# A mixing and convolution kernel: the order and queue of its first loads, dummy matmuls, and an early table load

## The chip, the cores and the metric

The kernel runs on one core of one Trainium2 chip. The metric is the device time of one execution in microseconds. A core has five engines with instruction streams of their own (TensorE for matmuls, VectorE, ScalarE, GpSimd, and SyncE, here only an issuer of DMAs) and 16 DMA engines that all its queues share.

## The reference

The reference has two layers, each added to its input. The first mixes channels with one of 16 weight matrices, chosen for each batch element. The second is a long convolution along time whose kernel comes from 64 complex exponentials per channel.

```python
# x: (64, 128, 2048) float32; 16 weight matrices of (128, 128)
W = weights[condition]                        # condition: (64,) in 0..15
x = x + einsum('bct,bcd->bdt', x, W)
dt = exp(log_dt); A = -exp(log_A_real) + 1j * A_imag; dtA = A * dt[:, None]
Ct = (C[..., 0] + 1j * C[..., 1]) * (exp(dtA) - 1.0) / A
K = 2.0 * einsum('hn,hnl->hl', Ct, exp(dtA[:, :, None] * arange(2048))).real
y = causal_convolution(x, K)                  # by FFT in the reference
x = x + (y + x * D[:, None]) * (arange(2048) < length[:, None])[:, None, :]
```

## The kernel before, in words

The work has two phases. In the **mixing phase** a loop runs over the 64 batch elements ("samples"). For each, 1 MB of x is loaded (`x_f`, six buffers), multiplied on TensorE by a weight matrix with the identity added (`w_buf`, six buffers), copied in reversed order by ScalarE from PSUM to `stage` (four buffers), and stored to the scratch tensor `u_scratch` in DRAM. In the **second phase**, 64 pairs of channels are read back, and the convolution is made of matmuls with small Toeplitz matrices and a state of the exponentials. The second phase begins when the stores of all samples are done, but for some rows of the last four.

Each engine's stream is written out by hand, and they meet at semaphores. What matters for the first 60 us:

- **SyncE** (SP) issues, in this order, six loads for the natural parameters (`nat`, semaphore `s_in[0]`), the selector `cond_sb` (`s_in[3]`), `logs` (`s_in[1]`), the first six loads of x, two of `len_i` and one of `d_col` (`s_in[4]`). Then for each sample n it issues the load of sample n + 5 (from n = 1), waits for ScalarE's copies of sample n, and issues the store of sample n. So the seventh load of x stands behind the first store.
- **ScalarE** (ACT) issues the load of all weights, `w_f` (1 MB, `s_in[2]`). Then its loop waits for a sample's matmuls and for a free `stage`, and copies in two halves. After sample 4 it computes sines (`waves_of_turns`) for which it waits on VectorE (`s_turn`). Its table load is put in by the compiler ahead of the first activation.
- **GpSimd** (POOL) builds `ident` (which raises `s_const` to 2) and other constants. Then, after `w_f` and `cond_sb` are there, it reads the selector of each sample and adds the identity to its weight matrix, into `w_buf` (L348). At sample 30 it waits for `s_tab`, VectorE's tables, and builds some matrices ahead of the next `w_buf`.
- **TensorE** waits for `ident` and for the six `nat` loads, transposes four blocks (L392), and from then on mixes. Sample 1 waits, in addition, until VectorE has copied the four transposed blocks (`s_dve` at 4). From sample 30 on, five samples have small matmuls (`taps`, L400) ahead of their own, for which `s_tab` is needed. A sample's four float32 matmuls (L418) leave eight records in the trace.
- **VectorE** waits for the transposes, copies them (L643, L645), and then works through a long chain of small operations (the exponentials, powers and tables) until `s_tab` at L786, during the samples 0 to 29.

ScalarE's and SyncE's DMAs go to different queues: those of SyncE to q1, those of ScalarE to q10, GpSimd's to q0. The 16 DMA engines serve all.

Of the kernel before, what the change touches and what calls it, by code (L numbers as in the profile page):

```python
# [6 lines left out]
F32 = mybir.dt.float32  # L7
# [4 lines left out]
ACT = mybir.ActivationFunctionType  # L12

P = 128
NB, H, T = 64, 128, 2048
NC = 16
NM = 64
Q = 256
NJ = T // Q
JJ = 2  # L20
# [13 lines left out]

TAPS = 30
PIECES = 5
WAVES = 4
XS = 6
STAGES = 4
# [8 lines left out]
def ap(t, offset, dims, parts=P, first=0):  # L48

    width = 1  # L50
    for n in t.shape[1:]:
        width *= n
    return bass.AP(t, offset + first * width, [[width, parts]] + [list(d) for d in dims])


def build(nc, x, cond, length, w_in, log_dt, c_in, log_a, a_im, d_in, out):
# [6 lines left out]
    with ctx:  # L63
        def sb(name, shape, dt, where=ctx):
            return where.enter_context(nc.sbuf_tensor(name, shape, dt))
# [5 lines left out]
        cond_sb = sb("cond_sb", [1, NB], I32)  # L71
        len_i = sb("len_i", [P, 1], I32)
# [2 lines left out]
        row_f = sb("row_f", [P, 1], F32)  # L75
        pad = sb("pad", [P, 8], F32)
        d_col = sb("d_col", [P, 1], F32)
        ident = sb("ident", [P, P], F32)
        eyes = sb("eyes", [P, 2, NM], F16)
        lam_v = sb("lam_v", [P, H, 2, 2], F16)  # L80
# [31 lines left out]
        nat = [sb(f"nat{i}", [P, 2 * P], F32, making) for i in range(3)]  # L112
        logs = sb("logs", [P, 2, H], F32, making)
# [26 lines left out]
        bank = ctx.enter_context(nc.psum_tensor("bank", [P, 8, 512], F32))  # L140
# [55 lines left out]

        @block.sync
        def _(sp):
            sp.dma_start(nat[0][:, 0:NM], log_a[:, :]).then_inc(s_in[0], 16)
            sp.dma_start(nat[0][:, NM:P], log_a[:, :]).then_inc(s_in[0], 16)  # L200
            sp.dma_start(nat[1][:, 0:NM], a_im[:, :]).then_inc(s_in[0], 16)
            sp.dma_start(nat[1][:, NM:P], a_im[:, :]).then_inc(s_in[0], 16)
            sp.dma_start(nat[2][:, 0:P], c_in.rearrange("h n c -> h (n c)")).then_inc(s_in[0], 16)
            sp.dma_start(nat[2][:, P:2 * P], c_in.rearrange("h n c -> h (n c)")).then_inc(s_in[0], 16)
            sp.dma_start(cond_sb[:, :], cond.rearrange("(a b) -> a b", a=1)).then_inc(s_in[3], 16)
            sp.dma_start(logs[:, 0, :], log_dt.partition_broadcast(P)).then_inc(s_in[1], 16)

            def load_x(n):
                wait(sp, s_mm, n - XS + 1)
                sp.dma_start(x_f[n % XS][:, :], x[n, :, :]).then_inc(s_x[n % XS], 16)  # L210

            def store_u(n, first, last, s):
                dst = bass.AP(u_dram, first * ROWS * NG * Q + n * NG * Q,
                              [[ROWS * NG * Q, last - first], [NB * NG * Q, JJ], [1, NG * Q]])
                sp.dma_start(dst, stage[n % STAGES][first:last, :, :, :].rearrange("p j a t -> p j (a t)"))\  # L215
                    .then_inc(s, 16)

            for n in range(XS):
                load_x(n)
            for j in range(JJ):  # L220
                sp.dma_start(len_i[j * NB:(j + 1) * NB, :], length.rearrange("(b a) -> b a", a=1),
                             allow_slow_non_contiguous=True).then_inc(s_in[4], 16)
            sp.dma_start(d_col[:, :], d_in.rearrange("(h a) -> h a", a=1)).then_inc(s_in[4], 16)
            for n in range(NB):
                if 1 <= n <= NB - XS:
                    load_x(n + XS - 1)
                sp.wait_ge(s_ev, 2 * (n + 1))
                if n < NB - LATE:
                    store_u(n, 0, H, s_us[n % STAGES])
                else:  # L230
                    store_u(n, 0, EARLY, s_early)

            def load_u(i, c, h):
                wait(sp, s_ov, 4 * (UN * i + c - 4) + 2 * h + 2)
                sp.dma_start(u_row[c % 4][:, h, :, :].rearrange("p g q -> p (g q)"),  # L235
                             bass.AP(u_dram, (2 * (UN * i + c) + h) * (ROWS * NG * Q), [[NG * Q, ROWS], [1, NG * Q]]))\
                    .then_inc(s_row[c % 4][h], 16)

            def load_toeplitz(i, c):
                wait(sp, s_out, 4 * (UN * i + c - 3))  # L240
                src = bass.AP(k_dram, (UN * i + c) * (4 * KROW), [[1, P], [KROW, 4], [1, Q]])
                sp.dma_start(toep[c % 4][:, :, :, :].rearrange("p h a t -> p (h a) t"), src)\
                    .then_inc(s_t[c % 4], 16)

            def transpose_g(i, c):

                for lo in (0, NM):
                    sp.dma_start(gt_sb[c % 2][:, :, :, :, lo:lo + NM].rearrange("p h a b m -> p (h a b) m"),  # L248
                                 g_sb[c % 4][NM - lo:P - lo, :, :, :].rearrange("p h a t -> p (h a t)"),
                                 transpose=True).then_inc(s_gt[c % 2], 16)  # L250

            def store_out(i, c, h):
                o = 2 * (c % 2) + h
                sp.wait_ge(s_ov, 4 * (UN * i + c) + 2 * h + 2)
                for j in range(JJ):
                    dst = bass.AP(out.tensor, (2 * (UN * i + c) + h) * T + j * Q,
                                  [[H * T, NB], [JJ * Q, NG], [1, Q]])
                    sp.dma_start(dst, o_sb[o][j * NB:(j + 1) * NB, :, :]).then_inc(s_store[o], 16)

            sp.wait_ge(s_g, 1)  # L260
            transpose_g(0, 0)
            sp.wait_ge(s_kd, 80)
            for r in range(STAGES):
                sp.wait_ge(s_us[r], 16 * len(range(r, NB - LATE, STAGES)))
            sp.wait_ge(s_early, 16 * LATE)
            for c in range(2):
                for h in range(2):
                    load_u(0, c, h)
                load_toeplitz(0, c)

            def slot(i, c):
                if c == EARLY // 2 - 2:
                    sp.wait_ge(s_late, 16 * LATE)
                if has(i, c + 2):
                    load_u(i, c + 2, 0)
                if has(i, c + 1):

                    wait(sp, s_st, 7 * (UN * i + c) - 6)
                    sp.sem_inc(s_go, 1)
                    sp.wait_ge(s_g, UN * i + c + 2)  # L280
                    sp.sem_inc(s_go, 1)
                    transpose_g(i, c + 1)
                if has(i, c - 2):
                    store_out(i, c - 2, 1)
                if has(i, c + 2):
                    load_u(i, c + 2, 1)
                    load_toeplitz(i, c + 2)
                if c == 0:
                    for n in range(NB - LATE, NB):
                        store_u(n, EARLY, H, s_late)  # L290
                if has(i, c - 1):
                    store_out(i, c - 1, 0)

            slots(sp, slot)
            for o in range(4):
                sp.wait_ge(s_store[o], 32 * (PAIRS // 2))
# [87 lines left out]

        @block.tensor
        def _(pe):
            pe.wait_ge(s_const, 2)
            pe.wait_ge(s_in[0], 96)
            srcs = [nat[0][:, 0:P], nat[1][:, 0:P],
                    ap(nat[2], 0, [[P, 2], [2, NM]]), ap(nat[2], 1, [[P, 2], [2, NM]])]  # L390
            for k, src in enumerate(srcs):
                last = pe.transpose(bank[:, 4 + k, 0:P], src, ident[:, :])  # L392
            last.then_inc(s_tr, 1)

            def taps(piece, b):
                if piece == 0:
# [8 lines left out]

            for n in range(NB):
                if n == 1:
                    pe.wait_ge(s_dve, 4)
                wait(pe, s_ev, 2 * (n - 1))
                piece = n - TAPS  # L410
                if 0 <= piece < PIECES:
                    taps(piece, 4 * (n % 2))
                pe.wait_ge(s_x[n % XS], 16 * (n // XS + 1))
                pe.wait_ge(s_w, n + 1)
                for k in (1, 2, 3, 0):
                    if k == 0 and 0 <= piece < PIECES:
                        pe.wait_ge(s_kl, piece + 1)
                    last = pe.matmul(bank[:, 4 * (n % 2) + k, :], w_buf[n % XS][:, :],  # L418
                                     x_f[n % XS][:, k * 512:(k + 1) * 512], start=True, stop=True)
                last.then_inc(s_mm, 1)  # L420
# [98 lines left out]

        @block.scalar  # L520
        def _(act):
            act.dma_start(w_f[:, :, :], w_in.rearrange("s c d -> c s d")).then_inc(s_in[2], 16)

            def waves_of_turns():
                act.wait_ge(s_turn, 1)
# [369 lines left out]
```

## Time and profile before

| | |
|---|---|
| median of 3 runs | 1099.62 us (1095.68 to 1100.15) |
| the profiled execution | 1099.54 us, its span 1097.7 us |
| mean granted TensorE clock | 0.984 |
| busy shares of the span | PE 91%, PEld 67%, DVE 70%, ACT 50%, POOL 46% |
| HBM read, written | 152.37 MB, 134.41 MB |

The span is what the profiler saw from the first to the last instruction; the execution's own time is 1.84 us longer. PE is TensorE's matmul, PEld its weight load, DVE is VectorE, ACT ScalarE, POOL GpSimd, SPq the issuing of DMAs on SyncE. Matmuls are pipelined and their ends are modelled, so starts and the distances between them are the better measure. The DMA share of a stretch is the mean over 16 engines and can exceed 1 by a little, since packets overlap.

### The profile page before, as it was taken

Reading aid. Unit: us, or ns where it says so; the run is one execution under the profiler, and the core shown is the slowest. Engines: PE = TensorE matmul, PEld = TensorE weight load, DVE = VectorE, ACT = ScalarE, POOL = GpSimd, SP = SyncE. Lnnn points to the kernel's source line nnn. Section 1 sums busy time; section 2 is a strip of 40 time slices with the busy share of each in tenths; the row PEclk is TensorE's granted clock in tenths of the full one; section 3 lists DMA queues with packets and bytes.
Section 4 is the critical chain, followed back from the end, with each engine's and each line's share of the span. In section 5 each row is a group of like instructions: output and inputs, shape, how many; then the busy total and the mean of one; then the engine's idle time right before and its main releaser. Section 6 shows DMA issues by size and latency. Waiting matters only on the chain.

```text
span 1097.7 us, 29010 instructions
## 1 busy us (share of the span) xinstructions
PE 996.0 (91%) x11526; PEld 731.3 (67%) x11526; DVE 770.1 (70%) x1710; ACT 547.3 (50%) x1163; POOL 502.4 (46%) x542
## 2 busy tenths in 40 slices
PE   6987789677756999999999999999999999999997
PEld 2332244232224788888888888888888888888886
DVE  6989920000004888888888888888888888888885
ACT  2633344334332555555555555555555555555553
POOL 2111043000204466656656656556666566565530
PEclk9999999999997999999999999999999999999999
DMA  9999999999989899999999999999999999999994
GB/s 334 415 425 421 425 421 423 376 424 424 423 320 312 179 220 249 228 218 234 215 234 230 222 238 225 221 232 218 239 229 226 235 230 229 226 226 234 221 214 117
DMA packets 220311, 305.48 MB, mean 278 GB/s; under 512 B 79938, under 2 KB 178626, under 8 KB 211986
## 3 DMA queue, kind: packets, MB, share of 16 engines
q1 hardware_dynamic: 219490, 302.37, 97.6%
q8 instruction: 94, 1.54, 0.6%
q10 hardware_dynamic: 528, 1.05, 0.4%
q14 instruction: 39, 0.32, 0.1%
q0 software_dynamic: 160, 0.20, 0.1%
HBM read 152.37 MB, written 134.41 MB: 261 GB/s over the span
## 4 chain that ended last, share of the span: by engine, by line
PE 67%; DMA 25%; ACT 4%; SPq 2%; issue 1%; DVE 1%; ACTq 0%
DMA u_scratch<-stage 24%; PE bank L479 15%; PE bank L488 15%; PE bank L444 13%; PE bank L430 10%; PE bank L456 7%; PE bank L485 5%; ACT stage L554 3%; PE bank L418 2%; DVE x_t L831 1%; DMA x_f<-in_x 1%; SPq L248 1%; SPq L215 0%; SPq L235 0%; DVE st_sb L821 0%
## 5 line engine op out<-in xcount | busy, mean ns | idle before, releaser
L479 PE MATMUL bank<-toep,u_t 128*128 128x192 f16 (+1 forms) x3072 | 344.7, 220 | 0.4
L816 DVE SCALAR_TENSOR_TENSOR u_t<-bank,u_t 128x512 f16<-128x512 f32 x256 | 176.3, 688 | 193.9 <-ACT u_t L567 191.8
L488 PE MATMUL bank<-g_sb,st_sb 128*128 128x256 f16 x1536 | 307.4, 274 | 0.0
L418 PE MATMUL bank<-x_f,w_buf 128*128 128x512 f32 x512 | 240.7, 618 | 64.1 <-ACT stage L554 52.7
L430 PE MATMUL bank<-ident,u_row 128*128 128x128 f32 x1024 | 280.9, 279 | 11.7 <-DMA u_row<-u_scratch 11.1
L575 ACT ACTIVATE st_sb<-bank 128x128 f16<-128x128 f32 x448 | 123.8, 276 | 289.2 <-PE bank L456 199.5
L479 PEld LDWEIGHTS bank<-toep,u_t 128*128 128x128 f16 x3072 | 232.0, 99 | 14.9 <-issue 0.4
L418 PEld LDWEIGHTS bank<-x_f,w_buf 128*128 128x128 f32 x512 | 95.8, 195 | 204.7 <-issue 110.6
L846 DVE COPY_PREDICATED o_sb<-mask,u_row 128x512 f32<-128x512 uint8 x256 | 205.7, 803 | 16.6 <-issue 16.6
L554 ACT ACTIVATE stage<-bank 128x1024 f32<-128x1024 f32 x128 | 123.9, 1021 | 174.0 <-DMA u_scratch<-stage 156.8
L485 PE MATMUL bank<-toep,x_t 128*128 128x64 f16 x2048 | 189.0, 193 | 0.3 <-issue 0.3
L340 POOL TENSOR_TENSOR lam_sb<-eyes,lam_v 128x512 f16<-128x512 f16 x64 | 75.5, 1179 | 238.2 <-PE bank L456 238.2
L567 ACT ACTIVATE u_t<-bank 128x512 f16<-128x512 f32 x256 | 152.2, 595 | 59.2 <-PE bank L430 48.5
L821 DVE TENSOR_TENSOR st_sb<-bank,st_sb 128x128 f16<-128x128 f32 x448 | 129.6, 289 | 57.3 <-ACT st_sb L575 53.6
L430 PEld LDWEIGHTS bank<-ident,u_row 128*128 128x128 f32 x1024 | 146.3, 144 | 21.4 <-issue 13.1
L485 PEld LDWEIGHTS bank<-toep,x_t 128*128 128x128 f16 x2048 | 158.2, 98 | 0.5 <-issue 0.4
L444 PE MATMUL bank<-u_t,gt_sb 128*128 128x448 f16 x768 | 156.0, 353 | 0.2
L583 ACT ACTIVATE o_sb<-bank 128x512 f32<-128x512 f32 x256 | 153.3, 599 | 4.1 <-PE bank L488 4.0
L488 PEld LDWEIGHTS bank<-g_sb,st_sb 128*128 128x128 f16 x1536 | 149.6, 98 | 6.2
L456 PE MATMUL bank<-st_sb,lam_sb 128*128 128x64 f16 x2304 | 130.8, 193 | 9.6 <-DVE st_sb L821 9.2
L348 POOL TENSOR_TENSOR w_buf<-w_f,ident 128x128 f32<-128x128 f32 x64 | 33.1, 521 | 221.1 <-PE bank L418 215.6
L456 PEld LDWEIGHTS bank<-st_sb,lam_sb 128*128 128x128 f16 x2304 | 107.9, 98 | 38.3 <-issue 14.9
(122 smaller groups left out, 842.9 us busy)
## 6 DMA issues: line engine op xcount, KB each, us to landing
x_f<-in_x SPq DMA_DIRECT2D x64, 1024.0 KB, 19.6
u_row<-u_scratch SPq DMA_DIRECT2D x128, 512.0 KB, 5.8
out<-o_sb SPq DMA_DIRECT2D x256, 256.0 KB, 4.0
u_scratch<-stage SPq DMA_DIRECT2D x60, 1024.0 KB, 17.7
toep<-k_scratch SPq DMA_DIRECT2D x64, 256.0 KB, 5.6
u_scratch<-stage SPq DMA_DIRECT2D x4, 896.0 KB, 10.2
gt_sb<-g_sb SPq DMA_TRANSPOSE x128, 5.3
u_scratch<-stage SPq DMA_DIRECT2D x4, 128.0 KB, 4.7
```

What stands on the lines that cost most here:

```text
L418: last = pe.matmul(bank[:, 4 * (n % 2) + k, :], w_buf[n % XS][:, :], x_f[n % XS][:, k * 512:(k + 1) * 512], start=True, stop=True)
L430: last = pe.transpose(bank[:, 4 + q, g * P:(g + 1) * P], u_row[c % 4][:, h, g, tb * P:(tb + 1) * P], ident[:, :])
L444: last = pe.matmul(bank[:, h, 0:(NJ - 1) * NB], gt_sb[c % 2][:, h, a, 1 - tb, :], u_t[c % 4][:, h, tb, b, 0:(NJ - 1) * NB], start=(m == 0) ...
L456: last = pe.matmul(bank[:, h, j * NB:(j + 1) * NB], lam_sb[c % 2][:, h, a, :, :].rearrange("p k m -> p (k m)"), st_sb[c % 2][:, h, b, j * ...
L479: pe.matmul(bank[:, y, col + tb * P + NM:col + Q], u[:, h, tb, a, rows_], t[:, h, b, NM:Q - tb * P], start=first, stop=False, skip_group_c ...
L485: pe.matmul(bank[:, y, col + tb * P:col + tb * P + NM], x_t[c % 2][:, h, tb, rows_], t[:, h, b, 0:NM], start=False, stop=False, skip_group ...
L488: last = pe.matmul(bank[:, y, col:col + Q], st[:, h, a, gr * ROWS:(gr + 1) * ROWS], g[:, h, b, :], start=False, stop=(m == 2), skip_group_ ...
L554: act.activation(stage[n % STAGES][:, j, :, :].rearrange("p a (b t) -> p a b t", t=P), mixed[:, j, :, :, ::-1], ACT.Copy).then_inc(s_ev, 1)
L567: act.activation(u_t[c % 4][:, q // 2, q % 2, 0, :], bank[:, 4 + q, :], ACT.Copy, scale=US)\
L583: act.activation(o_sb[o][:, 2 * (v % 2):2 * (v % 2) + 2, :].rearrange("p g t -> p (g t)"), bank[:, 2 + v % 2, :], ACT.Copy, scale=1.0 / (U ...
L816: dve.scalar_tensor_tensor(out=t[:, q // 2, q % 2, 1, :], in0=bank[:, 4 + q, :], scalar=US, in1=t[:, q // 2, q % 2, 0, :], op0=MUL, op1=SU ...
L846: dve.copy_predicated(o_sb[2 * (c % 2) + v // 2][:, g2, :].rearrange("p g (b t) -> p (g b) t", t=P), mask[:, g2, :].rearrange("p g (b t) - ...
```

## The change

The loads of the small inputs leave SyncE's stream, so that the six loads of x are its first. ScalarE issues them all: `cond_sb` first, then `w_f`, then the rest in their old order. TensorE no longer begins with the transposes: it waits for `ident` only, runs 16 matmuls of `ident` with itself into a PSUM bank that nobody reads, mixes sample 0, and transposes ahead of sample 1. ScalarE gets an activation of one column that nobody reads, behind its DMAs, so that its table is loaded there.

```diff
+RUNUP = 16
@@ allocations
+        act_in = sb("act_in", [P, 1], F32)
@@ def _(sp)
-            sp.dma_start(nat[0][:, 0:NM], log_a[:, :]).then_inc(s_in[0], 16)
...
-            sp.dma_start(nat[2][:, P:2 * P], c_in.rearrange("h n c -> h (n c)")).then_inc(s_in[0], 16)
-            sp.dma_start(cond_sb[:, :], cond.rearrange("(a b) -> a b", a=1)).then_inc(s_in[3], 16)
-            sp.dma_start(logs[:, 0, :], log_dt.partition_broadcast(P)).then_inc(s_in[1], 16)
@@ behind the six load_x(n)
-            for j in range(JJ):
-                sp.dma_start(len_i[j * NB:(j + 1) * NB, :], length.rearrange("(b a) -> b a", a=1),
-                             allow_slow_non_contiguous=True).then_inc(s_in[4], 16)
-            sp.dma_start(d_col[:, :], d_in.rearrange("(h a) -> h a", a=1)).then_inc(s_in[4], 16)
@@ def _(pe)
             pe.wait_ge(s_const, 2)
-            pe.wait_ge(s_in[0], 96)
-            srcs = [nat[0][:, 0:P], nat[1][:, 0:P],
-                    ap(nat[2], 0, [[P, 2], [2, NM]]), ap(nat[2], 1, [[P, 2], [2, NM]])]
-            for k, src in enumerate(srcs):
-                last = pe.transpose(bank[:, 4 + k, 0:P], src, ident[:, :])
-            last.then_inc(s_tr, 1)
+            for _ in range(RUNUP):
+                pe.matmul(bank[:, 0, 0:P], ident[:, :], ident[:, :], start=True, stop=True)
@@ the loop over samples
             for n in range(NB):
                 if n == 1:
+                    pe.wait_ge(s_in[0], 96)
+                    srcs = [nat[0][:, 0:P], nat[1][:, 0:P],
+                            ap(nat[2], 0, [[P, 2], [2, NM]]), ap(nat[2], 1, [[P, 2], [2, NM]])]
+                    for k, src in enumerate(srcs):
+                        last = pe.transpose(bank[:, 4 + k, 0:P], src, ident[:, :])
+                    last.then_inc(s_tr, 1)
                     pe.wait_ge(s_dve, 4)
@@ def _(act)
+            act.dma_start(cond_sb[:, :], cond.rearrange("(a b) -> a b", a=1)).then_inc(s_in[3], 16)
             act.dma_start(w_f[:, :, :], w_in.rearrange("s c d -> c s d")).then_inc(s_in[2], 16)
+            act.dma_start(nat[0][:, 0:NM], log_a[:, :]).then_inc(s_in[0], 16)
...
+            act.dma_start(logs[:, 0, :], log_dt.partition_broadcast(P)).then_inc(s_in[1], 16)
+            for j in range(JJ):
+                act.dma_start(len_i[j * NB:(j + 1) * NB, :], length.rearrange("(b a) -> b a", a=1),
+                              allow_slow_non_contiguous=True).then_inc(s_in[4], 16)
+            act.dma_start(d_col[:, :], d_in.rearrange("(h a) -> h a", a=1)).then_inc(s_in[4], 16)
+
+            act.wait_ge(s_const, 2)
+            act.activation(act_in[:, :], ident[:, 0:1], ACT.Copy)
```

## Rows read from the trace of the kernel before

**Rows 1.** The page: DMA share and rate in 40 slices, and the chain by line.

```profile
DMA  9999999999989899999999999999999999999994
GB/s 334 415 425 421 425 421 423 376 424 424 423 320 312 179 220 249 228 218 234 215 234 230 222 238 225 221 232 218 239 229 226 235 230 229 226 226 234 221 214 117
...
DMA u_scratch<-stage 24%; PE bank L479 15%; PE bank L488 15%; PE bank L444 13%; PE bank L430 10%; PE bank L456 7%; PE bank L485 5%; ACT stage L554 3%; PE bank L418 2%; DVE x_t L831 1%; DMA x_f<-in_x 1%; SPq L248 1%; SPq L215 0%; SPq L235 0%
```

**Rows 2.** Stretches: busy time (instructions) of each engine, granted clock, DMA share, GB/s.

```profile
1.00:2.00 1.00, 0.00 (x0) 0.00 (x0) 0.00 (x0) 0.00 (x0) 0.59 (x4) 1.00 0.10 22
2.00:3.00 1.00, 0.00 (x0) 0.00 (x0) 0.00 (x0) 0.00 (x0) 0.65 (x7) 1.00 0.65 78
3.00:8.00 5.00, 0.00 (x0) 0.00 (x0) 0.00 (x0) 0.00 (x0) 1.66 (x8) 1.00 1.02 289
8.00:20.00 12.00, 9.63 (x17) 4.38 (x18) 9.51 (x27) 1.77 (x2) 3.35 (x7) 1.00 1.01 421
...
22.00:30.00 8.00, 8.00 (x20) 3.61 (x19) 7.68 (x7) 4.80 (x6) 1.42 (x3) 1.00 0.95 320
```

**Rows 3.** Timeline to 24 us: start, duration, engine, line, operation.

```profile
0.81 0.85 ACTq L522 DMA_DIRECT2D w_f<-in_L_cond_weights  x1
...
4.33 2.80 SPq L210 DMA_DIRECT2D x_f<-in_x  x6
...
9.21 0.45 POOL L348 TENSOR_TENSOR w_buf<-w_f,ident 128x128 f32<-128x128 f32 x1 [3.77 <-issue]
9.60 0.29 DVE L643 COPY logs<-bank 128x128 f32<-128x128 f32 x1 [9.60 <-PE bank L392]
...
11.46 24.05 PE L418 MATMUL bank<-x_f,w_buf 128*128 128x512 f32 x48 [1.90 <-DMA x_f<-in_x]
...
18.22 1.28 ACT L554 ACT_TABLE_LOAD   x1 [17.45 <-PE bank L418]
...
21.48 0.60 SPq L215 DMA_DIRECT2D u_scratch<-stage  x1
...
21.99 1.49 DVE L660 TENSOR_TENSOR waves<-waves,wide 128x1152 f32<-128x1152 f32 x1
```

**Rows 4.** Issues from 0 to 20 us: the last number is us to landing.

```profile
w_f<-in_L_cond_weights ACTq DMA_DIRECT2D x1, 0.5 KB, 6.9
```

**Rows 5.** DMA queues from 3 to 5, 5 to 7 and 8 to 20 us: packets, MB, share.

```profile
q10 hardware_dynamic: 297, 0.61, 97.4%
q1 hardware_dynamic: 5, 0.00, 0.3%
...
q10 hardware_dynamic: 213, 0.41, 74.0%
q1 hardware_dynamic: 447, 0.15, 34.4%
...
DMA packets 701, 5.05 MB, mean 421 GB/s; under 512 B 75, under 2 KB 85, under 8 KB 85
```

**Rows 6.** PE in one stretch (clock before the share), and the first matmuls.

```profile
42.00:43.00 1.00, 1.00 (x3) 0.50 1.09 459
...
8.47 1.09 PE L392 MATMUL bank<-ident,nat 128*128 128x128 f32 x4 [8.47 <-DMA nat<-in_L_cond_C]
```

**Rows 7.** The chain in order of time: start, duration, what.

```profile
41.09 5.41 PE bank L418 x8
```

**Rows 8.** Timelines from 138 to 163 us, of GpSimd and TensorE.

```profile
138.72 0.68 POOL L359 MEMSET st_sb<- 128x256 f16 x2 [13.30 <-DVEq L786]
...
148.03 0.86 POOL L348 TENSOR_TENSOR w_buf<-w_f,ident 128x128 f32<-128x128 f32 x2
...
157.29 1.76 PE L400 MATMUL bank<-beta_re,k_lhs 128*16 128x16 f32 x64
```

**Rows 9.** Issues from 60 to 300 us: the last number is us to landing.

```profile
u_scratch<-stage SPq DMA_DIRECT2D x48, 1024.0 KB, 17.7
...
k_scratch<-k_body POOLq DMA_DIRECT2D x4, 32.0 KB, 6.9
```

More of the change, by code:

```diff
@@ L198, in _ @@
         def _(sp):
-            sp.dma_start(nat[0][:, 0:NM], log_a[:, :]).then_inc(s_in[0], 16)
[L200 to L203, printed above, removed]
-            sp.dma_start(nat[2][:, P:2 * P], c_in.rearrange("h n c -> h (n c)")).then_inc(s_in[0], 16)
-            sp.dma_start(cond_sb[:, :], cond.rearrange("(a b) -> a b", a=1)).then_inc(s_in[3], 16)
-            sp.dma_start(logs[:, 0, :], log_dt.partition_broadcast(P)).then_inc(s_in[1], 16)
             def load_x(n):
@@ L521, in _ @@
         def _(act):
+            act.dma_start(cond_sb[:, :], cond.rearrange("(a b) -> a b", a=1)).then_inc(s_in[3], 16)
             act.dma_start(w_f[:, :, :], w_in.rearrange("s c d -> c s d")).then_inc(s_in[2], 16)
+            act.dma_start(nat[0][:, 0:NM], log_a[:, :]).then_inc(s_in[0], 16)
+            act.dma_start(nat[0][:, NM:P], log_a[:, :]).then_inc(s_in[0], 16)
+            act.dma_start(nat[1][:, 0:NM], a_im[:, :]).then_inc(s_in[0], 16)
+            act.dma_start(nat[1][:, NM:P], a_im[:, :]).then_inc(s_in[0], 16)
+            act.dma_start(nat[2][:, 0:P], c_in.rearrange("h n c -> h (n c)")).then_inc(s_in[0], 16)
+            act.dma_start(nat[2][:, P:2 * P], c_in.rearrange("h n c -> h (n c)")).then_inc(s_in[0], 16)
+            act.dma_start(logs[:, 0, :], log_dt.partition_broadcast(P)).then_inc(s_in[1], 16)
[5 more added lines that the diff above has]
+            act.activation(act_in[:, :], ident[:, 0:1], ACT.Copy)
             def waves_of_turns():
```

## The prediction

> **What bounds the kernel now.** First the page's chain, with its line of DMA busy shares and the rates below it [rows 1]. A quarter of the span (24%) hangs on stores of the stage, and the tenths of the DMA line stand at 9 for the first eleven slices of 27.4 us, some 300 us. So the mixing phase is bound by the 16 DMA engines (the later phase, where the DMA rate is near 230 GB/s, by TensorE). A change to the first 30 us can help only by filling time in which the DMA engines are not at full rate.
>
> The table by stretches says how much of that there is [rows 2]. Full rate is about 424 GB/s. From 0 to 8 us 1.54 MB were moved (0.022 + 0.078 + 5 x 0.289), where full rate gives 3.39 MB: 4.4 us lost. About 2 us of it are the start, before any packet; most of the rest is the price of small packets, with the engines busy (share 1.02 from 3 to 8 us), and stays with the bytes. Only the shares missing from 1 to 3 us (0.90 and 0.35) can be shortened. From 22 to 30 us the rate is 320: 104 x 8 / 424 = 1.97 us lost. The slices after it stand at 415 to 425, with few exceptions late in the phase.
>
> The timeline says why there is a hole at 22 us [rows 3]. The six loads of x are issued by 7.1 us and, by the rate, used up about 22.4 us. The next ones stand in SP's queue behind the first store, at 21.48. Before that store lie eight matmul records from 11.46 to 18.2, ScalarE's table load of 1.28 us and its copies of 1.94 us (19.5 to 21.48, less the handing over). Later a sample takes TensorE about 3.45 us ((24.05 - 6.8) / 5, from the 48 records) and the DMA engines 2 x 1.049 MB / 424 = 4.94 us, so a queue builds up behind them.
>
> **The change part by part.**
>
> *Loads of x first.* SyncE's first issue is at about 0.8 us, as w_f's on ScalarE. The first packet of any kind comes near 1.9 us (share 0.10 from 1 to 2 us), and those of x are of 8 KB, so the engines fill at once: of the missing 0.90 and 0.35 about 0.4 us is won (bounds 0 and 0.7). All the bytes stay, so the queue runs dry at 22.4 - 0.4 = 22.0 us.
>
> *The small loads on ScalarE.* Here I see the price. No sample starts without the weights: w_f landed at 7.71 (0.81 + 6.9 [rows 4]), and GpSimd had the first w_buf at 9.66 [rows 3], 1.95 us later. Before the change w_f met almost no rival: from 3 to 5 us its queue q10 had 297 packets in 97.4% of the time, 2 x 16 x 0.974 / 297 = 0.105 us each, and q1 had 5 [rows 5]. Afterwards q1 is full of 8 KB packets of x, each 0.315 us (12 x 16 x 1.01 / 616: the 701 of 8 to 20 us less 85 small ones [rows 5], with the share of [rows 2]). How two queues share an engine is what the sum hangs on. Nearest is the stretch from 5 to 7 us: both queues have packets and both move (213 and 447, the latter small), and q10 falls from 297 to 213. I take turns packet by packet. w_f has 512 / 16 = 32 packets on each engine, so it needs 32 x (0.105 + 0.315) = 13.4 us from about 3 us, or 12.4 if part of the small packets' cost hides under the large ones. I take 13, and half a microsecond to the landing: w_f lands at 16.5 us, with bounds 7.7 (undisturbed) and 21 (only when the x loads have let go, near 22). First matmul: 16.5 + 1.95 = 18.4 us against 11.46.
>
> The Trainium skill, page "DMA: Bandwidth & Descriptors", section "Queues, rings and completion order", says that each engine goes round robin between the queues that it has work for, a packet at a time. By that rule the landing is this 16.5 and the time this forecast; sharing in equal bytes would land w_f near 8.6 us and give the first rival's time. In no row of before do both queues have large packets, so this trace neither confirms nor refutes it.
>
> *16 matmuls on ident.* Ident is there within the first 2 us. A mixing matmul leaves two records, so these are 32; each takes between 0.21 us (a quarter of the 0.85 us spacing from 11.46 to 18.2, where a record has 512 columns) and 0.27 us (the four transposes with ident, 1.09 us [rows 6]). They end between 8 and 11 us. Only TensorE stands behind them, and it waits longer for the weights, so they cost nothing. They pay only if the clock is still up at 18.4 us. After a pause of 2.15 us the granted clock was 0.50 from 42 to 43 us (1.2 GHz) [rows 6], and eight records took 5.41 us instead of 3.45 [rows 7]. The pause here is 7 us or more. I count the clock as fallen: 6.1 us for the first sample (bounds 5.4 and 6.8, the two cold samples of before). It ends at 24.5.
>
> [...]
>
> *Table fetched early.* 1.28 us leave the path of the first store [rows 3]. ScalarE has 12 DMAs to issue ahead of it, one at 0.85 and eleven at about 0.47 (2.80 / 6 [rows 3]), 6.0 us; the table comes at about 9 and is needed at 24.5: hidden. First store: 24.5 + 0.1 + 1.94 = 26.5 us against 21.48.
>
> *Transposes moved behind sample 0.* They wait for six small loads queued behind w_f on q10, some 16 packets beside the last of x, then the rest, about 21.5 us: hidden under sample 0. Then 1.1 us of transposes [rows 6] and four vector copies of about 0.33 us (0.29 and a gap), now on TensorE's path: 2.4 us, in which nothing else can run there. Sample 1 goes from 26.9 to 30.3, its store out at 32.4 us.
>
> *What is late next.* VectorE starts at 25.6 instead of 9.60 [rows 3], 16 us later. It hands over s_tab at 154.6 instead of 138.6; GpSimd needs 9.4 us from there to the weights of sample 31, 164 instead of 148.0 [rows 8]. TensorE came to sample 31 at 157.3 [rows 8] and would stall a little; but the DMA engines have 17.7 us of work queued there [rows 9], and nothing shows at them until the delay is some 22 us plus the shift of mixing itself. ScalarE's wait for the turns at sample 4: they were done 13.9 us after VectorE's start (21.99 + 1.49 - 9.60 [rows 3]), so at 39.5, and ScalarE gets there at 42.7: nothing.
>
> **The sum.** Dry at 22.0; the first store's packets come 1.3 us after its issue, at 27.8: 5.8 us. That pair lasts 4.94 us, to 32.7; the next comes at 33.7: 1.0 us. Before, the dry spell itself was only 22.4 to 22.8, yet 1.97 was lost, so starting up again costs about 1.5 us: 1.5. Lost 8.3, less the 1.97 of before, less the 0.4 of the start: +5.9 us. From there mixing is bound by the DMA engines as before, and all the rest moves with it. The profiled execution took 1099.54 us (its span 1097.7 and 1.84 around it), 0.1 below the median of 1099.62; so the predicted time is 1105.4 us. This case alone: 1102.5 (w_f 1.5 us sooner, clock up sooner, a smaller restart) to 1108.5.
>
> **The rivals.**
> *Early weights (the faster side).* If w_f lands by about 11 us, shared by bytes or because its descriptors hold up those of x, TensorE starts at 10 to 13, the first store leaves before 21 and the hole at 22 closes: -1.97 - 0.4 = -2.4 us, 1097.1. For it: q1 had 5 packets in the 2 us in which w_f ran [rows 5], though small loads had been issued on it by then, so w_f can hold others up. Against: x[0] goes first. It decides at a landing of about 11.5 us, where the first store is no later than before.
> *Weights after x.* If q1 keeps the engines while it has packets, w_f lands at 21, the first matmul is at 23, the first store at 31; dry for 10.3 us, with 1.0 and 1.5: 12.8 - 1.97 - 0.4 = +10.4, 1110. Against: stores of k_scratch on q0 landed after 6.9 us while those on the full q1 took 17.7 [rows 9].
> *VectorE's chain too late.* If the small loads land 12 us or more later than I say, the cover at sample 31 is gone, and each further microsecond costs one: some 1108.
> *The clock stays up.* Late weights with 2.7 us less: 1102.7; rows 6 speak against it.
>
> **How the numbers follow.** Packet by packet with a fallen clock 0.54, clock up 0.04, early weights 0.29, after x 0.10, VectorE late 0.03. What a measurement of this kernel can tell from no change is about 0.5%, 5.5 us, and the likeliest case lies across that bound, a little more than half of it above. Slower: 0.29 + 0.10 + 0.03 = 0.42. Faster by 5.5 us is more than the two recoverable losses together (2.4 us), so only 0.03, for a gain that I don't see; the same 0.55. The range reaches down over the early case, to 1096.5, and up to 1109.5, which leaves out most of the case after x.
>
> **What would show it.** Right: w_f lands near 16.5 us; the first mixing record near 18 us, records 0.85 us apart, the granted clock 0.50 there; a DMA share under 0.5 between 22 and 28 us; VectorE's first copy near 26 us; s_tab near 155. Wrong: w_f landed by 11 us, a first store before 21 us and no hole in the DMA line; or a hole of over 8 us.

## The result, and the profile after

The changed kernel takes 1108.70 us (median of 11 runs, 1101.85 to 1114.13), the kernel before 1099.28 (11 runs, 1095.65 to 1103.24). The ratio is 1.0092, 95% interval 1.0065 to 1.0119: slower by 10.1 us, 7.1 to 13.1. The predicted time was 1105.4 us with a range of 1096.5 to 1109.5, so the median lies inside, 3.3 us above the prediction. By the bound of 5.5 us that the prediction set for telling a change, the likeliest of its three outcomes, "the same" with 0.55, did not come; "slower" (0.42) did. The profiled execution took 1112.61 us.

The page of the changed kernel, the same three lines as [rows 1]:

```profile
DMA  7899999999999999999999999999999999999994
GB/s 276 339 422 424 423 423 422 377 425 423 423 377 284 170 222 216 238 230 220 232 221 229 231 231 229 229 230 230 228 221 224 224 230 236 226 225 235 222 216 115
...
DMA u_scratch<-stage 24%; PE bank L471 15%; PE bank L480 15%; PE bank L436 13%; PE bank L422 10%; PE bank L448 7%; PE bank L477 5%; ACT stage L561 3%; PE bank L410 2%; DMA w_f<-in_L_cond_weights 2%; SPq L237 1%; DVE x_t L838 1%; SPq L224 0%
```

The first two slices of the DMA line fell from 9 9 to 7 8, from 334 and 415 GB/s to 276 and 339. From the third slice on the rates are those of before until the end of mixing has shifted. And the chain has a new member: 2% of the span hangs on the load of w_f. Its stretches, with the columns of [rows 2]:

```profile
1.00:2.00 1.00, 0.47 (x2) 0.47 (x3) 0.00 (x0) 0.17 (x1) 0.59 (x4) 1.00 0.79 107
2.00:3.00 1.00, 1.00 (x7) 1.00 (x7) 0.00 (x0) 0.00 (x0) 0.65 (x7) 1.00 0.46 139
3.00:8.00 5.00, 4.91 (x27) 4.71 (x26) 0.00 (x0) 0.00 (x0) 1.66 (x8) 1.00 1.01 412
8.00:20.00 12.00, 0.00 (x0) 0.00 (x0) 0.00 (x0) 1.37 (x2) 0.00 (x0) 0.60 1.02 387
...
22.00:30.00 8.00, 6.64 (x13) 2.72 (x12) 1.32 (x5) 1.85 (x2) 2.26 (x5) 0.67 0.06 8
30.00:57.00 27.00, 24.85 (x58) 10.89 (x59) 25.61 (x38) 16.95 (x19) 5.49 (x7) 1.00 0.96 372
```

In the stretch from 22 to 30 us, where the kernel before moved 320 GB/s [rows 2], the DMA share is 0.06. The hole reaches beyond 30 us:

```profile
22.50:31.50 9.00, 7.64 (x16) 3.38 (x15) 2.69 (x9) 1.94 (x2) 1.95 (x5) 0.73 0.02 7
```

The chain in order of time (start, duration, what) names what was waited for:

```profile
1.52 18.33 DMA w_f<-in_L_cond_weights
...
21.44 6.61 PE bank L410 x8
28.05 0.47 PE bank L398 x4
```

The timeline of the changed kernel shows the steps that answer to [rows 3]:

```profile
0.75 3.26 SPq L203 DMA_DIRECT2D x_f<-in_x  x6
...
1.53 6.37 PE L379 MATMUL bank<-ident 128*128 128x128 f32 x32 [1.53 <-POOL ident L291]
...
2.45 5.76 ACTq L516 DMA_DIRECT2D nat<-in_L_cond_log_A_real  x1
...
18.62 1.28 ACT L529 ACT_TABLE_LOAD   x1 [17.13 <-issue]
...
21.44 6.61 PE L410 MATMUL bank<-x_f,w_buf 128*128 128x512 f32 x8 [13.54 <-POOL w_buf L337]
...
28.54 0.29 DVE L650 COPY logs<-bank 128x128 f32<-128x128 f32 x1 [28.54 <-PE bank L398]
...
30.12 0.64 SPq L208 DMA_DIRECT2D u_scratch<-stage  x1
```

w_f landed at 19.85 us (1.52 + 18.33) instead of 7.7, the first mixing matmul came at 21.44 instead of 11.46, the first store at 30.12 instead of 21.48, while the six loads of x had been issued by 4.0 us and were used up at 22.

**A marker for the rest of the study.** From 57 us on both kernels move 418 GB/s until 300 us, so what the first 57 us cost can be read at one instruction near the end of mixing: the store issued right behind the last load of x, that of sample 58. It is issued at 302.73 us before and at 312.63 after, +9.9 us. (The expectations below call it the 60th store; it is the 59th, the same instruction in every kernel.) The marker repeats to within 1 us (312.6 and 311.8 in two traces of the changed kernel, 308.4 and 308.7 in two of another), while the slowest and fastest of 11 executions are 7.6 us apart before and 12.3 after.

### The profile page after: what moved, and what is told of

Read it like the earlier page. It is cut to its first block, busy times and chain, and to the rows that moved or that the text cites. A ratio compares the mean times of both kernels' runs of the same rounds, so it can differ in the third digit from the quotient of the medians.

```text
span 1110.8 us, 29074 instructions
## 1 busy us (share of the span) xinstructions
PE 999.2 (90%) x11558; PEld 735.9 (66%) x11558; DVE 768.1 (69%) x1710; ACT 547.5 (49%) x1164; POOL 500.8 (45%) x542
## 4 chain that ended last, share of the span: by engine, by line
PE 67%; DMA 25%; ACT 3%; issue 2%; SPq 1%; DVE 1%; POOLq 0%; ACTq 0%; POOL 0%
DMA u_scratch<-stage 24%; PE bank L471 15%; PE bank L480 15%; PE bank L436 13%; PE bank L422 10%; PE bank L448 7%; PE bank L477 5%; ACT stage L561 3%; PE bank L410 2%; DMA w_f<-in_L_cond_weights 2%; SPq L237 1%; DVE x_t L838 1%; SPq L224 0%; SPq L208 0%; DVE st_sb L828 0%
## 5 line engine op out<-in xcount | busy, mean ns | idle before, releaser
L410 PE MATMUL bank<-x_f,w_buf 128*128 128x512 f32 x512 | 237.4, 611 | 78.5 <-ACT stage L561 54.2
## 6 DMA issues: line engine op xcount, KB each, us to landing
u_scratch<-stage SPq DMA_DIRECT2D x60, 1024.0 KB, 17.7
```

## The experiments

Each is timed against runs of the kernel before on its own chip. The first five columns of numbers are read in the trace of one execution, in us but for the rate; the last two are the marker's distance to before's, in that one trace of the kernel before, and the difference in time worked out from the ratio, with its 95% interval.

| kernel | w_f landed | first mixing matmul | first store | 22 to 30 us, GB/s | marker | marker - before's | time - before's |
|---|---|---|---|---|---|---|---|
| before | 7.7 | 11.46 | 21.5 | 320 | 302.7 | | |
| changed | 19.8 | 21.44 | 30.1 | 8 | 312.6 | +9.9 | +10.1 (7.1 to 13.1) |
| 1 loads and transposes only | 19.7 | 21.29 | 30.9 | 7 | 312.4 | +9.7 | +12.1 (8.9 to 15.1) |
| 2 x in 2 KB packets | 13.8 | 15.40 | 24.2 | 325 | 305.0 | +2.3 | +3.1 (1.0 to 5.2) |
| 3 w_f ahead | 14.3 | 16.25 | 24.0 | 228 | 308.4 | +5.7 | +10.0 (6.6 to 13.4) |
| 4 before, plus matmuls and table | 7.5 | 11.93 | 17.7 | 416 | 300.2 | -2.6 | -1.9 (-3.9 to 0.1) |
| 5 before, plus table | 7.4 | 11.46 | 19.7 | 413 | 300.2 | -2.5 | -2.7 (-5.2 to -0.2) |
| 6 before, plus matmuls | 7.4 | 11.41 | 20.2 | 368 | 301.5 | -1.3 | -1.0 (-3.0 to 1.0) |
| 7 changed, w_f in SyncE's queue | 7.4 | 10.44 | 17.9 | 422 | 301.1 | -1.6 | -0.3 (-2.6 to 2.1) |
| 8 kernel 4 with x[0] first | 9.9 | 13.29 | 19.0 | 417 | 300.5 | -2.2 | -2.6 (-4.9 to -0.4) |
| 9 changed, again | 19.8 | 21.40 | 29.8 | 9 | 311.8 | +9.0 | +8.2 (5.0 to 11.4) |
| 10 w_f ahead of cond_sb | 18.7 | 20.90 | 28.8 | 5 | 310.2 | +7.4 | +8.2 (5.4 to 11.2) |
| 11 four x loads held | 11.8 | 13.39 | 21.4 | 419 | 304.4 | +1.7 | +0.9 (-1.4 to 3.1) |
| 12 kernel 3 again | 14.4 | 16.27 | 24.1 | 216 | 308.7 | +6.0 | +7.0 (4.3 to 9.7) |

**1. The loads and the transposes without the other two parts.** The changed kernel less these lines:

```diff
-            for _ in range(RUNUP):
-                pe.matmul(bank[:, 0, 0:P], ident[:, :], ident[:, :], start=True, stop=True)
...
-            act.wait_ge(s_const, 2)
-            act.activation(act_in[:, :], ident[:, 0:1], ACT.Copy)
```

> The changed kernel without the 16 matmuls and without the early activation; order and queues of the loads, and the place of the transposes, stay changed. My theory (w_f takes turns with 8 KB packets of x and lands late; all else is a consequence): w_f lands at 19.8 us as in the changed kernel, first mixing matmul at 21.4, records 0.85 us apart as there, the table load of 1.28 us now lies between sample 0 and its copy, first store at 31.4 instead of 30.1 us, DMA engines dry from 22.5 to about 33, time 1.3 us above the changed kernel's, about 10.5 us above before. Rival (the unread matmuls or ScalarE's added activation cost something themselves): the hole shrinks and the time comes down by 2 us or more.

w_f landed at 19.7 and the marker stands at 312.4, as in the changed kernel. So the loss is in the loads (with the transposes behind them); the two other parts neither cost nor gave anything there. The table load did come back ahead of the first copy, yet the first store is only 0.8 us later than in the changed kernel: sample 0 ended 0.5 us sooner here (21.29 + 6.30 = 27.59 against 28.05). The second store leaves at 35.10, not later than in the changed kernel (35.56), and the marker is not later at all, so the 1.3 us that I expected on top did not show.

**2. Smaller packets of x.** Same bytes, same queue:

```diff
             for n in range(XS):
-                load_x(n)
+                for k in range(4):
+                    sp.dma_start(x_f[n][:, k * 512:(k + 1) * 512], x[n, :, k * 512:(k + 1) * 512])\
+                        .then_inc(s_x[n], 16)
...
-                pe.wait_ge(s_x[n % XS], 16 * (n // XS + 1))
+                pe.wait_ge(s_x[n % XS], 16 * (n // XS + 4))
```

> The changed kernel with each of the first six loads of x issued as four loads of 512 columns, so that its packets have 2 KB instead of 8 KB; same bytes, same queues, same order. My theory (turns packet by packet): each of w_f's 32 rounds costs 0.21 us instead of 0.42, so w_f needs 6.7 us instead of 13.4 and lands at 13 to 14 us instead of 19.8. The smaller packets can cost up to 48 x 0.105 = 5 us of DMA time in the six loads, so the time itself may lie anywhere from 1101 to 1107. Rival (w_f waits for bytes or for the whole of the x loads queued ahead): it lands at 19 to 24 us.

w_f landed at 13.8 instead of 19.8 us, the time that I had given for turns by packets, although the same bytes of x were to go through q1. The time came out at +3.1 us. But this is no clean test of the turns, for two things changed beside the size of the packets. SyncE issues x more slowly (24 loads by 17.5 us), so that q1 was not always full: from 7 to 8 us q10 had 105 packets and q1 only 68. And w_f's first packets came between 4.5 and 5 us, over 1 us sooner than in the changed kernel. Experiment 11 is the cleaner test.

**3 and 12. The descriptors of w_f first.**

```diff
+            sp.wait_ge(s_const, 2)
             for n in range(XS):
                 load_x(n)
...
-            act.dma_start(cond_sb[:, :], cond.rearrange("(a b) -> a b", a=1)).then_inc(s_in[3], 16)
             act.dma_start(w_f[:, :, :], w_in.rearrange("s c d -> c s d")).then_inc(s_in[2], 16)
+            act.dma_start(cond_sb[:, :], cond.rearrange("(a b) -> a b", a=1)).then_inc(s_in[3], 16)
```

> The changed kernel, but ScalarE issues w_f before cond_sb, and SyncE waits for ident (1.5 us) before its first load of x, so that w_f's descriptors are issued before those of x. My theory: the 3.3 us by which w_f's first packet came later than I had said (6.3 against 3 us) are its place behind the x loads in the making of descriptors: its first packet comes near 3 us, it then takes turns, and lands near 16.5 us; first matmul 18.3, first store 27, DMA hole of about 6 us, time 3 us below the changed kernel's, about 1105.5. Rival 1 (the late start has another cause, such as ScalarE's queue itself): first packet near 6.3, landing 19.8. Rival 2 (the order of issue decides which queue is served, not turns): w_f lands near 8 us and the hole is gone.

> Experiment 3's kernel again, with more rounds: its three timed runs lay 5 to 8 us above its profiled one, so its time (8.5 us above before) and its 60th store (5.7 us later than before) disagree. If the trace is typical, w_f lands near 14.3 again, the 60th store is at about 308.4 and the time is 5.7 us above before, about 1102.5; if the profiled execution was a lucky one, the store lies nearer to 311 and the time again 8 to 10 us above before.

Both traces agree with each other to 0.3 us. The first packets of w_f come in the stretch from 2 to 3 us, where the changed kernel has none before 6, and then the two queues move packet for packet. The queues of this kernel, from 2 to 3 and from 7 to 10 us (packets, MB, share):

```profile
q10 hardware_dynamic: 62, 0.13, 50.6%
...
q1 hardware_dynamic: 121, 0.94, 82.2%
q10 hardware_dynamic: 118, 0.24, 21.5%
```

w_f lands at 14.3, 2.2 us sooner than I had said and 5.5 sooner than in the changed kernel. Not all of that is the start of its packets, which comes some 3.5 us sooner (about 2.5 instead of 6): the first ones, 62 in the stretch from 2 to 3 us, also met none of x. The marker gained only 4.2 us on the changed kernel, though the first store came 6.2 us sooner. The timeline shows the next thing in line: the transposes now wait 1.45 us for the last load of c_in, and sample 1 starts at 25.37, so the second store goes out only at 31.07.

```profile
23.34 0.67 PE L399 MATMUL bank<-ident,nat 128*128 128x128 f32 x4 [1.45 <-DMA nat<-in_L_cond_C]
25.37 7.13 PE L411 MATMUL bank<-x_f,w_buf 128*128 128x512 f32 x16 [1.36 <-DVE ci L653]
```

The repeat's time is +7.0 us (4.3 to 9.7), an interval that holds the marker's +6.0, so the trace was typical. The first time's +10.0 (6.6 to 13.4) rests on four runs, and its interval leaves out the marker's +5.7; why, no run shows.

**4. The two other parts on the kernel before.** Its loads stay as they were, and ten more unread matmuls behind the transposes, which the change does not have, keep TensorE from pausing for long:

```diff
             pe.wait_ge(s_const, 2)
+            for _ in range(16):
+                pe.matmul(bank[:, 0, 0:P], ident[:, :], ident[:, :], start=True, stop=True)
             pe.wait_ge(s_in[0], 96)
...
             last.then_inc(s_tr, 1)
+            for _ in range(10):
+                pe.matmul(bank[:, 0, 0:P], ident[:, :], ident[:, :], start=True, stop=True)
...
             act.dma_start(w_f[:, :, :], w_in.rearrange("s c d -> c s d")).then_inc(s_in[2], 16)
+            act.wait_ge(s_const, 2)
+            act.activation(act_in[:, :], ident[:, 0:1], ACT.Copy)
```

> The kernel before, its loads untouched, with only the two parts of the change that are not loads: 16 matmuls on ident ahead of the transposes and ten more behind them (so that no pause of 2 us is left before x[0] lands), and ScalarE's early activation behind its load of w_f. My theory: w_f lands at 7.7 and x[0] at 11.4 as before; the mixing records of sample 0 stand 0.43 us apart instead of 0.85 and no table load follows, so the first store is out at 16.9 instead of 21.48 us, the hole from 22 to 30 us closes (415 GB/s or more instead of 320), and the time falls by 2 us to about 1097.3. Rival (the hole at 22 us isn't made by the late first store): the rate there stays at 320 and the time at 1099.3.

The stretch from 22 to 30 us of this kernel, against the 320 of [rows 2]:

```profile
22.00:30.00 8.00, 8.00 (x20) 3.52 (x19) 7.65 (x7) 4.47 (x5) 1.66 (x3) 1.00 1.03 416
```

The hole is closed and the marker is 2.6 us earlier; the time is 1.9 us lower, with an interval that just reaches zero (-3.9 to 0.1). The first store left at 17.7 us, 0.8 later than I had said; 0.5 of it is x[0], which landed at 11.9 instead of 11.4. So the hole of the kernel before was made by the late first store, and the two parts are good for what can be had, if the loads are left alone.

**5 and 6. One of the two parts at a time** on the kernel before: in 5 the last two lines of the diff of experiment 4, in 6 its first two.

> The kernel before with ScalarE's early activation alone. My theory: the first sample is mixed as before (11.46 to 18.2 us, 0.85 us between records), its copy starts at 18.3 instead of 19.5, first store at 20.2 instead of 21.5 us; most of the hole from 22 to 30 us closes, the 60th store of the stage is issued 1 to 1.5 us earlier than before (302.7), the time is 1 us lower. Rival (the early table gives nothing, since the next stores depend on TensorE): 60th store at 302.7, time unchanged.

> The kernel before with the 16 unread matmuls alone, ahead of the transposes. From about 9 us, behind the transposes, TensorE pauses 2.4 us until x[0] has landed at 11.4; in two traces the granted clock fell about 2.5 us after the last matmul. My theory: the clock is up at 11.46 or falls shortly after it: if it stays, the first store is out at 18.2 us and the 60th at 300.5, if it falls for some us, at 19.5 to 21 and 301 to 302.7. Rival (the clock doesn't matter at the start, as the DMA engines bound all): the 60th store at 302.7 whatever the records' distance.

The early table alone gives the marker of both together (300.2): with the first store at 19.7 us there is already no dry spell (413 GB/s). That is 2.5 us, more than the 1 to 1.5 that I had expected. The 16 matmuls alone close the hole only in part (368 GB/s). Their marker is 1.3 us earlier, little more than the 1 us to which it repeats, and their time can't be told from no change. The trace of kernel 6 says why it is so little:

```profile
11.41 3.40 PE L420 MATMUL bank<-x_f,w_buf 128*128 128x512 f32 x4 [2.55 <-DMA x_f<-in_x]
...
11.00:12.00 1.00, 0.59 (x1) 0.92 1.07 451
12.00:13.00 1.00, 1.00 (x3) 0.50 1.02 426
...
15.00:16.00 1.00, 1.00 (x3) 0.88 1.01 426
```

There is a pause of 2.55 us between the transposes and the first sample, and the granted clock is 0.50 (1.2 GHz) from 12 to 15 us, with four records in 3.40 us, 0.85 apart.

**7. The changed kernel with w_f in SyncE's queue.** One line moved:

```diff
+            sp.dma_start(w_f[:, :, :], w_in.rearrange("s c d -> c s d")).then_inc(s_in[2], 16)
             for n in range(XS):
                 load_x(n)
...
-            act.dma_start(w_f[:, :, :], w_in.rearrange("s c d -> c s d")).then_inc(s_in[2], 16)
```

> The changed kernel with one line moved: w_f is issued by SyncE ahead of the x loads, in their queue. My theory (a queue is served in order, two queues take turns by packets): w_f has 32 packets for each engine and meets only small packets of q10, so it lands at 7 us instead of 19.8; the first matmul is at 9 us and the clock, up from the 16 unread ones, gives records 0.43 us apart; the six nat loads take their turns mostly with w_f's packets and the rest with those of x, landing at about 12, so sample 1 starts at 13 to 14; the first store is out before 16, no hole at 22 us, 60th store at 300 us, time 2.5 us below before. Rival (the loss of the change lies in the moved transposes or the late nat loads as well): a hole or a late VectorE chain remains and the time stays above before.

This line alone takes away the whole loss: w_f at 7.4, no hole (422 GB/s), the marker 11.5 us below the changed kernel's and 1.6 below before's. The moved transposes and the other small loads on q10 are thus no loss that counts. Together with experiment 3, where w_f was issued ahead of x but on the other queue and landed at 14.3, it also shows that being first is not enough: the queue matters. The first matmul waited for x[0] instead, until 10.44, after a pause of 2.35 us, and was mixed at the low clock after all; so the first store is at 17.9 and not before 16. The time is that of before (-0.3, -2.6 to 2.1), where I had expected 2.5 us less.

**8. One load of x ahead.** Kernel 4 with the load of x[0] as SyncE's first:

```diff
+            sp.dma_start(x_f[0][:, :], x[0, :, :]).then_inc(s_x[0], 16)
             sp.dma_start(nat[0][:, 0:NM], log_a[:, :]).then_inc(s_in[0], 16)
...
-            for n in range(XS):
+            for n in range(1, XS):
                 load_x(n)
```

> Experiment 4's kernel (loads as before, unread matmuls, early activation) with x[0] alone issued ahead of the small loads on SyncE. My theory: one load of x ahead costs w_f 8 turns of 0.315 us instead of the 32 of the changed kernel, since behind x[0] q1 holds small packets: w_f lands near 9.5 to 10 us (7.7 without it, 19.8 in the changed kernel), first matmul at 11 to 12, no hole, 60th store at about 300, time as in experiment 4 within 0.5 us. Rival (a load of x ahead holds w_f off as a whole, whatever its size): w_f lands after 13 us and the first matmul with it.

w_f landed at 9.9 us, as I had said, and 2.4 us later than in kernel 4. But the reason was another than turns. The queues from 4.5 to 5 and from 5 to 5.5 us:

```profile
q1 hardware_dynamic: 96, 0.13, 72.0%
q10 hardware_dynamic: 5, 0.01, 5.2%
...
q10 hardware_dynamic: 75, 0.15, 78.8%
q1 hardware_dynamic: 86, 0.03, 24.7%
```

Up to 4.5 us q10 had no packet at all. By then 0.92 MB had gone through q1, and of its next 96 packets 82 were small ones: w_f began when the 1.05 MB of x[0] were through, and met hardly any packet of x. In kernel 4, as in the kernel before, its packets begin between 2 and 3 us. So the 2.4 us are a later start. That is the rival's reason, though not its time (after 13 us), and this run says nothing on the turns.

**9. The changed kernel again.**

> The changed kernel once more, on the chip of this batch, to see how much of its trace repeats. My theory (what decides is fixed by the order of issue): w_f lands at 19.5 to 20.1 us, the DMA engines are dry from 22.5 to 31.5, 60th store at 312 to 313 us, time 10 us above before. Rival (w_f's landing differs from one execution to the next, and the 12 us between the changed kernel's fastest and slowest run come from there): it lands more than 1 us away from 19.8 and the 60th store moves with it.

w_f at 19.8 again, the first matmul within 0.04 us, the marker at 311.8. The two profiled executions of this kernel took 1112.61 and 1106.18 us; of these 6.4 us, 0.9 lie ahead of the marker, the rest behind it.

**10. w_f ahead of cond_sb alone**, the second half of the diff of experiment 3.

> The changed kernel with w_f ahead of cond_sb on ScalarE, and nothing else (SyncE doesn't wait, as it did in experiment 3). My theory: descriptors are made in the order of issue, whichever engine issues; w_f's issue now ends near 1.7 us with two loads of x ahead of it instead of three or four, so its first packet comes between 3.5 and 5 us (2.3 in experiment 3, 6.3 in the changed kernel), it then needs 12 to 13 us, and lands at 16 to 18 us; 60th store between 308.4 and 312.6. Rival (what held w_f's first packet off was SyncE's issuing at all, not the number of loads ahead): 6.3 and 19.8 us.

A miss: w_f landed at 18.7 and not at 16 to 18, its first packets between 5.0 and 5.5 us. The order on ScalarE alone is worth 1.1 us; the rest of experiment 3's gain needed SyncE's wait beside it.

**11. Four of the six loads of x held back.**

```diff
             for n in range(XS):
+                if n == 2:
+                    sp.wait_ge(s_in[2], 16)
                 load_x(n)
```

> The changed kernel, but SyncE issues only x[0] and x[1] at the begin and the next four loads of x after w_f has landed. My theory: w_f has 16 turns with packets of x (0.42 us each) and 16 without (0.105), 8.4 us from a first packet near 4 us: it lands at 12 to 13.5 us, first matmul at 14 to 15.5, first store at 23 to 24. The other x loads are issued at about 13 us and keep the engines until 24 or so; the hole is 1 to 2 us in place of 9; 60th store at 303 to 305 us, time 0 to 3 us above before. Rival (turns aren't what holds w_f): landing at 16 us or later.

w_f landed at 11.8 and the first store left at 21.4, sooner than I had said by 0.2 and 1.6 us. The turns are what holds w_f: with two of the six loads of x in q1 it lands 8.0 us sooner. When these two were through, w_f had the engines to itself, here from 8 to 9 us:

```profile
q10 hardware_dynamic: 156, 0.32, 106.9%
q1 hardware_dynamic: 7, 0.00, 0.4%
```

That is 156 packets in 1 us, where beside x it had 40. There is no hole at 22 us (419 GB/s), but the held loads are missed earlier: before 20 us this kernel moves 284 GB/s, the kernel before 330. The marker is at +1.7, the time at +0.9 (-1.4 to 3.1). The first packets of w_f still came between 5.5 and 6 us. So the third to the sixth load of x have no part in its late start.

## Why the prediction was right, and where it was off

**The turns.** Right, and shown. In the changed kernel from 7 to 10 us (packets, MB, share):

```profile
q1 hardware_dynamic: 130, 0.93, 79.7%
q10 hardware_dynamic: 128, 0.26, 23.0%
```

130 packets of one queue against 128 of the other, 0.93 MB against 0.26. On 16 engines 128 packets are 8 turns in 3 us, 0.375 us a turn, where I had 0.42 (13 us in all after a small deduction). From the first packet at 6 us to the landing w_f took 13.8 us, where I had 13.5. The Trainium skill, page "DMA: Bandwidth & Descriptors", section "Queues, rings and completion order", gives this order, packet by packet between the queues; this trace agrees, with 130 to 128.

**Where w_f's first packet stands.** This is the term that was mis-sized. I had it near 3 us, from the kernel before, where q10's packets began there; in the changed kernel they begin at about 6 us (18 packets from 6 to 7 us), 3 us later, behind x[0] and about four tenths of x[1] (1.46 MB in q1 by then), and ScalarE's next issue was held for 5.76 us. The landing was 19.85 instead of 16.5 us, and with it all that follows: the first matmul 21.44 against 18.4, the first store 30.1 against 26.5. Wherever x[0] was issued before w_f, w_f's packets began between 4.5 and about 6 us: from 4.5 to 5 with one load of x issued ahead of w_f (kernel 8), from 5 to 5.5 with a second one issued during w_f's issue (kernel 10), from 5.5 to about 6 with two ahead of it (kernels 9 and 11 and the changed kernel). Kernel 3, where w_f was issued first, has them from about 2.5 us. The start thus moves with what of x is issued ahead of w_f, but the second load of x moved it by 1 us and not by the 2.5 that such a load takes at full rate. Why it is so late stays open; no run separates the causes.

**The weights' way to TensorE.** Predicted 1.95 us, measured 21.44 - 19.85 = 1.59.

**The clock.** Right, and shown. The 32 records of the unread matmuls end at 7.9 us, inside the 8 to 11 but for 0.1; no matmul follows for 13.5 us, and in the changed kernel the granted clock is 0.65 from 10 to 11 us and 0.50 from 11 us. The first sample took 6.61 us (predicted 6.1, bounds 5.4 and 6.8).

```profile
10.00:11.00 1.00, 0.00 (x0) 0.65 1.01 383
11.00:12.00 1.00, 0.00 (x0) 0.50 0.99 365
```

**The table.** Hidden in the changed kernel, as predicted, though much later than I said (18.62 instead of 9): ScalarE's DMA issues took until then. ScalarE then waited 8.0 us for sample 0; a table later by more than that would have been on the path.

**The transposes.** Sample 1 started 29.86 - 28.05 = 1.8 us behind sample 0, against 2.4; the wait for the nat loads was hidden, as said. Experiment 3 shows that this was near to failing: with w_f 5.5 us sooner they were the ones waited for.

**VectorE's chain and sample 31.** Right. It started at 28.54 instead of 9.60. GpSimd had the tables at 157.14 and built the weights of sample 31 only from 166.45, when TensorE had begun with the taps of that sample at 166.23:

```profile
157.14 0.68 POOL L348 MEMSET st_sb<- 128x256 f16 x2 [22.95 <-DVEq L793]
...
166.45 0.87 POOL L337 TENSOR_TENSOR w_buf<-w_f,ident 128x128 f32<-128x128 f32 x2
```

The DMA rate from 160 to 180 us is 422 GB/s with a share of 1.02: the delay of 18.4 us stayed under the queue's cover of 22.

**The sum.** Against a full rate of 424 GB/s, the changed kernel loses from 22 to 57 us 8 x 416 / 424 + 27 x 52 / 424 = 11.2 us, the kernel before 1.9 (at 320 and then 425). The difference, 9.3, had been 8.3 - 1.97 = 6.3 in the sum. The dry spell alone is some 9.2 us, from about 22.1 to 31.4, where I had 5.8: 3.4 more, which is w_f's late landing. What follows it, 2.0 us, is a little less than the 1.0 and 1.5 of the sum. The gain at the start, put at 0.4: before 20 us the two lose 3.6 and 4.4 us, and from 20 to 22 us the changed kernel gives 0.4 of these back (331 GB/s); so it is as small as predicted. With w_f's landing put right by 3.3 us the sum gives +9.2, 1108.7. By the rates the loss is 8.9 us; the marker shows +9.9, and the 1.0 between them is no more than the 1 us to which the marker repeats.

**Its own sign of being wrong.** The prediction had named "a hole of over 8 us" as a sign that it was wrong. The hole was 9.2 us, so by its own words that sign came, and it points at the same term: the landing at 19.85 instead of 16.5 makes up the excess. The other numbers that it gave to look for, near 16.5, 18, 26 and 155, came at 19.85, 21.44, 28.54 and 157.1, each late by 2 to 3.5 us; the records 0.85 us apart and the granted clock of 0.50 came as said.

**The rivals.** "Early weights" was wrong for the change as it stands. Experiment 7 reaches its condition by one line, but its gain of 2.4 us only in part (marker -1.6, time -0.3, -2.6 to 2.1); kernels 4, 5 and 8 gain 2.2 to 2.6 at the marker, though two of them do not have x first and had only the hole to close. Its turning point, a landing at 11.5 us, was well placed: in kernel 11 w_f landed at 11.8 and the first store left at 21.4, as before. "Weights after x" fell: w_f moved beside x from 6 us on, and landed before x was used up. What it gave as a time, 1110, is near the median only because w_f started late; that nearness is luck. "The clock stays up" and "VectorE too late" did not come.

**The chances.** With a forecast of +5.9 us, just above the bound of 5.5, the mis-sized start decided the side: +10 us is slower, and I had given that less than "the same". That the median still lies inside the range is owed to its upper end, 1109.5, 0.8 us above it.

## What to carry to other kernels

Two queues shared the DMA engines here by packets and not by bytes. Beside loads of 8 KB packets, a load of 2 KB packets got about a fifth of the bytes, so the load that everything waits for belongs in front, in the same queue. Look at what the first matmul needs (here 1 MB of weights, not x), and put nothing large beside it. And before adding unread matmuls to keep the clock up, read from the trace how long TensorE idles behind them. Here a cheap move of ScalarE's table load closed the hole alone (413 GB/s), while the matmuls alone closed it only in part (368).

## What the runs showed of the hardware that I had not expected

- How late a queue's first packet can be behind another's: w_f, whose issue on ScalarE ended at 2.4 us, had its first packets at about 6 us when SyncE's loads of x began at 0.75. They came at about 2.5 us in experiment 3, where w_f was issued at 0.81 and the loads of x from 1.51. ScalarE's next DMA issue took 5.76 us in the changed kernel and 2.02 in experiment 3; the one behind it took 0.50 and 0.36.
- How exactly two hardware queues took turns: 130 to 128 packets in 3 us, 121 to 118 in experiment 3, with a byte ratio of 3.6 and 3.9.
- The granted clock did not fall with the last matmul but some time behind it, and a matmul that had begun by then did not stop it. In the changed kernel the last matmul ends at 7.9 us and the clock is 0.65 from 10 to 11. In kernel 7 TensorE pauses for 2.35 us until 10.44, and the clock is 0.84 from 10 to 11 and 0.50 from 11 to 14; in kernel 6 it pauses for 2.55 us until 11.41, and the clock is 0.92 from 11 to 12 and 0.50 from 12 to 15. In kernel 4, with a pause of 0.76 us ahead of the first sample, it stays at 1.00.
- The granted clock reads 1.00 from the start of every trace, also in kernel 1 from 22 to 30 us, whose first records stand 0.85 us apart as at 1.2 GHz. So in these traces it says nothing ahead of its first change; there the distance between records tells the clock.
